# First norm's tokens of chunks 4 to 15 transposed through a DRAM scratch and VectorE instead of TensorE

## The reference

```python
x = x + attn(layernorm(x))
x = x + ffn(layernorm(x))

def attn(x):                       # d_inner 512, d_state 16, 4 taps
    xp, z = split(x @ w_in)        # 256 -> 2 x 512
    xc = silu(causal_depthwise_conv(xp, conv_w) + conv_b)
    h = h * 0.9 + 0.1 * (xc_t @ w_B)     # scan over time
    y = (h @ w_C) * silu(z)
    return y @ w_out               # 512 -> 256

def ffn(x):                        # 8 experts, top 2, chosen by the first token of a sequence
    idx = top_k(x[:, 0] @ Wr + br, 2)
    h = gelu(x @ W1[idx] + b1[idx])
    return sum(h @ W2[idx] + b2[idx]) / 2
```

## Time and profile before

| | |
|---|---|
| median of 3 runs | 560.03 us (559.35 to 561.41) |
| the profiled execution | 561.27 us, span 559.5 us |
| PE busy | 540.8 us (97%) |
| DVE busy | 461.2 us (82%) |
| ACT busy | 372.7 us (67%) |
| POOL busy | 342.7 us (61%) |
| mean granted TensorE clock | 0.991 of full |

### The profile page before, as it was taken

One profiled execution on the slowest core, in us unless ns is written; L12 is line 12 of the kernel. 1 busy time (PEld: TensorE's weight loads), 2 busy tenths in 40 slices (PEclk: granted clock), 3 DMA queues, 4 the chain that ended last, 5 costly groups with the idle time before them and its releaser, 6 DMA issues. The chain is left out here.

```text
span 559.5 us, 9918 instructions
## 1 busy us (share of the span) xinstructions
PE 540.8 (97%) x3196; PEld 470.5 (84%) x3196; DVE 461.2 (82%) x935; ACT 372.7 (67%) x626; POOL 342.7 (61%) x347
## 2 busy tenths in 40 slices
PE   7978998999999999999999999999999999999897
PEld 6757877888898888988888888888889888888886
DVE  5986979969997789968999689987899789794772
ACT  4755594676867767686776768667767766776343
POOL 4739659545776457673594647854586835653670
PEclk8989999999999999999999999999999999999899
DMA  8940101112021110302002120111203011020211
GB/s 252 301 146 2 37 2 57 57 39 76 2 68 47 57 56 0 112 0 94 19 14 99 37 75 0 61 52 37 75 0 112 0 43 34 1 75 1 77 37 39
DMA packets 35162, 32.09 MB, mean 57 GB/s; under 512 B 5442, under 2 KB 34626, under 8 KB 35010
## 3 DMA queue, kind: packets, MB, share of 16 engines
q1 hardware_dynamic: 33282, 31.48, 18.0%
q10 hardware_dynamic: 1856, 0.31, 0.3%
HBM read 23.39 MB, written 8.39 MB: 57 GB/s over the span
## 5 line engine op out<-in xcount | busy, mean ns | idle before, releaser
L659 DVE SCALAR_TENSOR_TENSOR conv<-blk,tap_w,conv 128x512 f32<-128x512 f32 x192 | 129.9, 742 | 10.2 <-ACT conv L446 9.0
L328 POOL TENSOR_TENSOR y_lo<-gate,y_hi 128x512 fp32r<-128x512 f32 x64 | 80.9, 1295 | 62.3 <-ACT y_hi L405 62.3
L299 POOL TENSOR_TENSOR xc_lo<-conv,xc_hi 128x512 fp32r<-128x512 f32 x62 | 78.0, 1274 | 55.2 <-ACT xc_hi L405 55.1
L839 PE MATMUL blk<-xn_hi,w_in_hi 128*128 128x512 f32 x252 | 102.8, 408 | 4.6 <-DVE conv L659 3.9
L840 PE MATMUL blk<-xn_hi,w_in_lo 128*128 128x512 f32 x252 | 100.6, 399 | 0.0
L844 PE MATMUL blk<-xn_lo,w_in_hi 128*128 128x512 f32 x252 | 80.0, 399 | 0.0
L580 DVE TENSOR_TENSOR hid_lo<-hid,hid_hi 128x512 fp32r<-128x512 f32 x64 | 51.1, 819 | 35.0 <-ACT hid_hi L405 35.0
L896 PE MATMUL tok<-w_hi,hid_hi 128*128 128x256 f32 x256 | 72.6, 284 | 2.2 <-DVE hid_lo L580 1.9
L896 PE MATMUL tok<-w_out_hi,y_hi 128*128 128x256 f32 x256 | 73.2, 286 | 0.3 <-POOL y_lo L328 0.3
L898 PE MATMUL tok<-w_out_hi,y_lo 128*128 128x256 f32 x256 | 72.3, 282 | 0.0
L897 PE MATMUL tok<-w_out_lo,y_hi 128*128 128x256 f32 x256 | 72.1, 282 | 0.0
(11 more groups left out here) (104 smaller groups left out, 1266.5 us busy)
## 6 DMA issues: line engine op xcount, KB each, us to landing
x_mid<-in_L_attn_x SPq DMA_DIRECT2D x32, 256.0 KB, 2.8
out<-x_mid SPq DMA_DIRECT2D x32, 256.0 KB, 2.8
x_in<-in_L_attn_x SPq DMA_DIRECT2D x14, 512.0 KB, 3.5
w_all<-in_L_ffn_W SPq DMA_DIRECT2D x2, 2048.0 KB, 13.4
b_all<-in_L_ffn_b SPq DMA_DIRECT2D x1, 1024.0 KB, 15.7
gate<-in_L_attn_w_in SPq DMA_DIRECT2D x2, 256.0 KB, 4.6
gate<-in_L_attn_w_in SPq DMA_DIRECT2D x1, 512.0 KB, 6.8
hid<-in_L_attn_w_out SPq DMA_DIRECT2D x1, 512.0 KB, 5.5
```

The costliest lines, as they stand in the source:

```text
L299: nc.gpsimd.tensor_tensor(xc_lo[:, j, :], conv[:, j, 0:CH], xc_hi[:, j, :].bitcast(F32), ALU.subtract).then_inc(xc_lo_set, 1)
L328: nc.gpsimd.tensor_tensor(y_lo[:, j, :], gate[:, j, :], y_hi[:, j, :].bitcast(F32), ALU.subtract).then_inc(y_lo_set, 1)
L659: nc.vector.scalar_tensor_tensor(cols, blk[j][:], tap_w[:, j, t:t + 1], cols, ALU.mult, ALU.add).then_inc(tap_added, 1)
L839: mm(dst, whi(k), his(k), start=(k == 0), stop=False)
```

## The change

For chunks 4 to 15 the transposes of the first norm leave PE. (Chunks 0 to 3 stay as they were.) The new path has six pieces:

1. POOL's `norm1` of chunk a + 1 (not a + 2) stands right behind `split_y`, at the start of the step, and writes `normed1` in an order grouped by 32 features.
2. SP stores `normed1` to a DRAM scratch `spill1` (512 KB) and reads it back in four DMAs (`regroup`, 128 KB each), one for each group of 32 partitions, so that partition (g, i) holds feature group g of tokens i, 32 + i, 64 + i, 96 + i of every tile.
3. DVE's `turn_squares` transposes all 32x32 blocks of `normed1` in place with one instruction of 128x1024.
4. ACT's `turn1_hi` reads `normed1` from SBUF, behind the gelus and not ahead of them.
5. POOL's `turn1_lo` (two subtractions of 128x512) stands at the end of the step; DVE's `turn1_lo` is gone for these chunks.
6. SP's order is changed: both stores of the last finished chunk, both refills, the spill, the fetch of chunk s + 2, the four reads back.

Beside it: the bias copies `b1_sel` go from DVE to ACT; `stats1` of chunk a + 2 is cut into pieces between the four `hidden_lo`; `edge` (3 columns of the convolution's halo) stands behind `scan`; the bank of `state_in` and `scan` is `turn1` instead of `tok1` from chunk 3 on, so `down` no longer waits for `scan` there, nor `state_in` for the residual.

```diff
@@ SP
-            def step(s, q, seq, ahead):
-                if ahead:
-                    fetch(s + 3)
+            def spill(c):
+                sp.wait_ge(norm1_ready, c + 1)
+                sp.dma_start(spill1.rearrange("p g c -> p (g c)"), normed1[:]).then_inc(spilled1, 16)
+
+            def regroup(c):
+                sp.wait_ge(spilled1, (c - 3) * 16)
+                for g in range(QUADS):
+                    sp.dma_start(normed1[g * SQ:(g + 1) * SQ, :].rearrange("i (q c) -> i q c", q=QUADS),
+                                 spill1[:, g, :].rearrange("(q i) c -> i q c", q=QUADS)).then_inc(regrouped1, 16)
+
+            def step(s, q, seq):
                 for h in range(2):
-                    store(s - 2, q, h)
-                    refill(s, q, h, seq)
+                    store(s - 3, 1 - q, h)
+                for h in range(2):
+                    refill(s - 1, 1 - q, h, seq - 1 if q == 0 else seq)
+                if not isinstance(s, int) or s + 1 <= LAST:
+                    spill(s + 1)
+                if not isinstance(s, int) or s + 2 <= LAST:
+                    fetch(s + 2)
+                if not isinstance(s, int) or s + 1 <= LAST:
+                    regroup(s + 1)
@@ POOL
             def norm1(c):
-                if not (isinstance(c, int) and c == 0):
+                if isinstance(c, int) and c <= 4:
                     pool.wait_ge(turned1, c * KD)
+                else:
+                    pool.wait_ge(t1_lo, c * KD)
...
+            def turn1_lo(c):
+                for k in range(KD):
+                    pool.wait_ge(t1_hi, c * KD + k + 1)
+                    nc.gpsimd.tensor_tensor(in_order(xn1_lo, k), regrouped(normed1, k),
+                                            in_order(xn1_hi, k).bitcast(F32), ALU.subtract).then_inc(t1_lo, 1)
...
+                if has_next(s, 1) and not third:
+                    pow1(a + 1)
+                    norm1(a + 1)
...
-                if has_next(s, 2):
-                    pow1(a + 2)
-                    norm1(a + 2)
+                if has_next(s, 1) and not third:
+                    turn1_lo(a + 1)
@@ ACT
+                else:
+                    act.wait_ge(squares1, c - 3)
+                    for k in range(KD):
+                        hi(in_order(xn1_hi, k), regrouped(normed1, k)).then_inc(t1_hi, 1)
...
+                    hi(b1_sel[:, t, :], b1_all[:, bass.ds(e, 1), :].rearrange("p o k -> p (o k)")).then_inc(b1_set, 1)
...
-                if has_next(s, 1) and not second:
+                if has_next(s, 1) and not second and on_pe(a + 1):
                     turn1_hi(a + 1)
...
                     gelus(f, q, half - 1)
+                if has_next(s, 1) and not on_pe(a + 1):
+                    turn1_hi(a + 1)
@@ DVE
+            def turn_squares(c):
+                dve.wait_ge(regrouped1, (c - 3) * QUADS * 16)
+                nc.vector.transpose(normed1[:], normed1[:]).then_inc(squares1, 1)
...
+            def hidden_lo_and_stats1(f, c):
+                hidden_lo(f, 0)
+                dve.wait_ge(x_loaded, c * 16)
+                for n in (0, 1):
+                    nc.vector.bn_stats(stats1_t[:, n, :], x_in[:, n, :])
+                hidden_lo(f, 1)
+                for n in (2, 3):
+                    ins = nc.vector.bn_stats(stats1_t[:, n, :], x_in[:, n, :])
+                ins.then_inc(stat1_step, 1)
+                hidden_lo(f, 2)
+                moments1(c)
+                hidden_lo(f, 3)
...
-                for t, e in enumerate(chosen):
-                    ins = nc.vector.tensor_copy(b1_sel[:, t, :], b1_all[:, bass.ds(e, 1), :].rearrange("p o k -> p (o k)"))
-                ins.then_inc(b1_set, 1)
...
+                elif has_next(s, 1):
+                    turn_squares(a + 1)
+                if has_next(s, 2) and not third:
+                    hidden_lo_and_stats1(f, a + 2)
...
                 if has_attn(s):
                     scan(a, q)
+                if has_next(s, 1):
+                    edge(a + 1, q == 1)
@@ PE
         def u_bank(a):
-            return turn[0] if isinstance(a, int) and a == 1 else tok[1]
+            if isinstance(a, int) and a < 3:
+                return turn[0] if a == 1 else tok[1]
+            return turn[1]
...
-                if has_next(s, 1):
-                    turns1(a + 1)
+                if third:
+                    turns1(3)
...
                 if has_attn(s):
-                    pe.wait_ge(mid_set, o * 2 + 2)
+                    if third:
+                        pe.wait_ge(mid_set, o * 2 + 2)
+                    else:
+                        pe.wait_ge(t2_lo, f * KD + KD)
                     state_in(a)
...
                     down(f, 0)
-                    if has_attn(s):
+                    if third:
                         pe.wait_ge(scanned, a + 1)
```

More of the change, by code:

```diff
@@ L256, in _ @@
             fetch(4)
+            step(3, 1, 1)
             with sp.Fori(0, LOOPED) as i:
-                step(i * 2 + 2, 0, i + 1, True)
-                step(i * 2 + 3, 1, i + 1, True)
-            for s in range(2 * LOOPED + 2, NC):
-                step(s, s % 2, s // 2, s + 3 <= LAST)
+                step(i * 2 + FIRST, 0, i + FIRST // 2)
+                step(i * 2 + FIRST + 1, 1, i + FIRST // 2)
+            for s in range(2 * LOOPED + FIRST, NC + 1):
+                step(s, s % 2, s // 2)
             for f in (NC - 2, NC - 1):
@@ L827, in turns2 @@
             def turns2(o):
-                if has_next(o, 2):
+                if isinstance(o, int) and o < 2:
                     pe.wait_ge(t1_lo, (o + 3) * KD)
+                else:
+                    pe.wait_ge(t2_lo, o * KD)
                 pe.wait_ge(norm2_ready, o * 2 + 2)
```

70 lines of the change are left out of this document (45 added, 25 removed).

## The result

| | kernel before | changed kernel |
|---|---|---|
| median of 19 runs each, us | 560.22 (559.35 to 563.07) | 558.54 (557.29 to 559.34) |
| profiled execution, us (its span) | 561.27 (559.5) | 558.54 (556.7) |
| ratio to before | 1 | 0.9962, 95% interval 0.9952 to 0.9972 |

By the ratio the change saves 2.1 us (1.6 to 2.7) where 8 were forecast: clear of no change, but less than the 0.5% that the prediction set for "faster".

The account below looks back on a forecast made before the run. PE, 97% busy, was taken as the bound, in even steps by a hair DVE too. Gains of 4.2 + 2.0 + 0.9 + 0.9 = 8.0 us off the profiled 561.27 gave 553.3, in medians 552.0; range 547.5 to 560.

Parts of the forecast that it names:

- rival B: Collisions of DVE's two-input work with turn1_lo take nearly all the gain in both kinds of step: 557.6 us, chance 0.20.
- odd steps: Six loop steps, 3 to 13: each gains 0.7 of PE's 0.87 us, together 4.2 us.
- even steps 4 to 12: Five loop steps: state_mix comes 0.4 us late, so each gains 0.4 and not 0.87, together 2.0 us.
- step 14: Even step with no statistics left to make: gains 0.87 us in full, 0.9 in the sum.
- step 2: DVE reaches the first hid_lo 1.1 us earlier without the bias copies: gains 0.9 us (0 to 1.1).
- PE's price of the transposes: Eight transposes cost PE 0.80 us plus 0.08 behind them, taken as 0.87 us in each of steps 3 to 14.
- The even step's price of the collisions: DVE's and POOL's two-input subtractions wait for each other near hid_lo and state_mix: 1.2 us (0.5 to 2.1).
- the slack of 0.8: Even step: DVE's state_mix is done at 353.4 and PE wants it at 354.20, leaving 0.8 us for contention with POOL.
- The DRAM trip and the transpose: Trip taken as 10 us (7.9 to 13.8), DVE's block transpose as 1.2 (1.1 to 2.7); both hidden at no cost.
- Rival D: DVE's block transpose takes 2.7 us, 0.8 late in five even steps: 4 us less gain, 556 us, chance 0.08.
- C: Data back from DRAM too late, beyond 11.1 us (odd) or 11.8 (even): slower, 570 us at 13 us, chance 0.14.
- By a hair bounded by DVE too: Kernel before, even step: bounded by PE and nearly by DVE, whose state_mix is ready 0.18 us before PE takes it.

Follow-up runs that it names:

- experiment 5: Changed kernel with POOL's two turn1_lo subtractions waiting until DVE has finished both halves of the second norm: 548.79 us, ratio 0.9781.
- experiment 11: Kernel before with only the bias copies b1_sel moved from DVE to ACT: 559.47 us, ratio 0.9972.
- experiment 3: Changed kernel with POOL's two turn1_lo subtractions cut from 512 to 32 columns for chunks 4 to 15, all waits kept: 547.74 us, ratio 0.9759.
- experiment 1: Changed kernel with POOL's two turn1_lo subtractions waiting until DVE has made state_mix: 549.91 us, ratio 0.979.
- experiment 2: Changed kernel with state_mix directly behind the scan, ahead of the edge copy and the second norm on DVE: 552.85 us, ratio 0.9842.
- experiment 4: Changed kernel with only the edge copy moved behind state_mix on DVE: 557.73 us, ratio 0.9945.
- experiment 10: Changed kernel with the four statistics in one piece ahead of the four hid_lo, not between them: 557.82 us, ratio 0.9942.
- experiment 12: Changed kernel with turn1_lo waiting for both halves of the second norm and the statistics in one piece ahead of hid_lo: 548.26 us, ratio 0.9776.
- Experiment 6: Kernel before with 2 instead of 8 first-norm transposes on PE for chunks 4 to 15, nothing in their place: 557.58 us, ratio 0.9931.
- experiment 8: Changed kernel with turn1_lo waiting for both halves of the second norm, and the trip through DRAM made twice: 576.20 us, ratio 1.0259.

## Why the prediction was wrong, and where it was right

The forecast was 552.0; the time was 558.54, near rival B's 557.6 and inside the range. By its terms, against the table of steps above:

| term | forecast, us | changed kernel | without the collision (experiment 5) |
|---|---|---|---|
| odd steps | -4.2 | -4.6 | -5.1 |
| even steps 4 to 12 | -2.0 | +3.6 | -4.8 |
| step 14 | -0.9 | +0.25 | -0.9 |
| step 2 | -0.9 | -1.0 | -1.6 |
| step 15 | 0 | +0.1 | 0 |
| sum | -8.0 | -1.6 | -12.3 |

- **PE's price of the transposes, 0.87 us: right.** Experiment 5's odd steps are 0.87 shorter (31.79 against 32.66). Its even steps (32.16) are 0.88 shorter than those of experiment 11 (33.04), where PE alone bounds the step.
- **The even step's price of the collisions: the step that failed.** I had put it at 1.2 us, 2.1 at the most, and only on operations with two SBUF inputs, `hid_lo` and `state_mix`. By that the edge and the half norm in between were 0.1 and 0.7 us long and out of harm's way. The measured delay is 1.77 us between scan and `state_mix`, all of it on the edge and the norm (0.7 and 1.0), and 0.6 on the fourth `hid_lo` (1.24), beside the bias additions: 2.3 us, over my upper end and on other instructions. Less the slack of 0.8 that makes 1.5 us late, and PE waited 1.40. DVE's own count up to the scan was sound: experiment 3, with the subtractions cut short, has nothing else changed and gives all the gain back. Against the forecast 5.6 us are missing here and 1.1 in step 14.
- **Step 14: the same, forgotten.** I said that it has no statistics left to make and so gains in full. But edge or statistics don't matter: the norm stands there too, and 33.04 became 33.29.
- **Odd steps: right in size, partly by luck.** 0.77 each where 0.7 was forecast. The norm is stretched by 1.0 us there as well, and `state_mix` comes 0.08 us ahead of PE. I had the slack at 0.7 us and the possible collision at 1.04, on the last `hid_lo`, and took the value between; the collision was full, on the norm, and the slack was 1.1 and just enough (experiment 5's odd steps are still 0.1 shorter).
- **Step 2: right in number by luck** (1.02 for 0.9). The bias copies, the cause by experiment 11, are worth 1.6 us there, over my upper end of 1.1; experiments 1, 3 and 5, with the same program up to that point, gain 1.6 too. In the changed kernel's trace a collision that I hadn't counted takes 0.6 back. Its rows, DVE's and POOL's:

```profile
82.48 1.32 DVE L667 TENSOR_SCALAR var_eps<-mean_var 128x4 f32<-128x4 f32 x1
...
82.48 1.29 POOL L349 TENSOR_TENSOR xc_lo<-conv,xc_hi 128x512 fp32r<-128x512 f32 x1
```

An operation on 4 elements a partition takes 1.32 us beside one subtraction. The two start within 0.02 us of each other in all these traces; in the changed kernel and experiments 2 and 4 DVE's is held, in experiments 1, 3, 5, 10 and 12 it takes 0.16.
- **The DRAM trip and the transpose: right that they cost nothing.** The trip took 7.2 us against 10 taken, under my lower end of 7.9, since I had 3.5 for the store, and it took 2.9. The transpose took 1.25 against 1.2. Rival D falls. For C the limits that I gave, 11.1 and 11.8, were measured as about 11.8 and 12.1.
- **"By a hair bounded by DVE too": right, and more than a hair's worth.** Experiment 6 shows that without the change's relief of DVE the even steps give nothing.
- **Rival B** came out in size, not in kind: it had both kinds of step lose their gain on two-input work. The odd steps kept theirs, and the even ones became slower than before.

The rule was at hand. The Trainium skill, "SBUF — State Buffer", in its part on who interferes with whom, says that `copy` and `tensor_scalar` can enter modes that use both of DVE's ports and then contend with GpSimd, as operations with two SBUF inputs do, and that whichever issues first blocks the other for its whole instruction. I had weighed only the half on two inputs. By the other half, the copy and the norm (SBUF to SBUF, one tensor input) can have to wait, and the statistics need not. The traces agree: 0.83 for 0.15, 1.44 for 0.40 on one instruction of the norm, and 0.40 unchanged. That these two ran in such a mode no run shows. The 1.07 us lost in the `hid_lo` of the kernel before showed one class of operations, and I didn't ask which others POOL would meet in its new place.

In experiment 5 even steps are 0.37 us longer than odd ones, although PE is busy in both. That is the router's score, four small matmuls that only even steps have: they stand where PE goes from the input projection to the output projection, and from the last matmul ahead of them to the second behind them it is 0.73 us, where in the odd step it is 0.35.

Left open: what the other bank for the scan is worth alone, and what decides which of two operations that start together is held.

## What to carry to other kernels

When work is given to GpSimd, list every VectorE instruction that its new place overlaps, and treat copies and scalar operations from SBUF to SBUF like those with two SBUF inputs: each can be held until the GpSimd instruction that it meets has ended, however short it is itself. Two short ones in a row met two subtractions in a row here, and the chain got longer by 1.7 us. Statistics, and products with one input in PSUM, took their usual time beside the same subtractions and can stand there instead. One wait that moves GpSimd's instructions behind the short critical ones turned a gain of 2 us into one of 12.

## What the runs showed of the hardware

- Beside GpSimd subtractions of 1.29 us each (two in a row), a VectorE copy of 12 elements a partition (0.15 us) took 0.83, a scalar operation on 256 elements (0.40) took 0.94 to 1.46, and a 64x512 subtraction (0.69) took 1.80 or 1.81. Each met one of the two: the copy ended with it, the scalar operations 0.15 us behind its end, the subtraction 0.55 behind.
- In step 2 a scalar operation on 4 elements a partition (0.16) took 1.32 us in the changed kernel's trace, and 0.16 in experiments 1, 3 and 5, each time started within 0.02 us of a GpSimd subtraction.
- Beside the same subtractions, statistics of 256 elements (0.40) and four multiplications with one input in PSUM (2.48) took their usual time. GpSimd lost little: 2.52 to 2.58 us for its two, 2.73 at the most (experiment 1).
- A block transpose of 128x1024 in f32 on VectorE takes 1.25 us, about what four statistics over the same elements took the earlier trace rows.
- 512 KB to DRAM and back in four reads of 128 KB, each into 32 partitions, takes 7.1 to 7.7 us from the end of the writer to the landing, of which 2.9 are the store and 2.8 the last read. Made twice in a row it took 14.1 to 15.8 (experiment 8).
